# First stage of a three-layer attention kernel: turning normalised tokens on TensorE, loading tokens ahead of scalars, and putting value groups among key groups

## The reference, cut to what matters

```python
x = x + attn_a(layernorm(x))      # 8 heads, two 64-wide halves each
x = x + ffn(layernorm(x))         # int4-quantised kernel plus low-rank part
x = x + attn_b(layernorm(x))      # 16 heads, causal, rotary
x = x + ffn(layernorm(x))

# start of attn_a
q = xn @ Wq.T;  k = xn @ Wk.T;  v = xn @ Wv.T
q1, q2 = l2norm(q halves);  k1, k2 = l2norm(k halves)
# scalars: exp(sum(lq1*lk1)) - exp(sum(lq2*lk2)) + 0.5, 15*sigmoid(raw)*(1 + 0.5*tanh(delta))
# ffn: scale = max|kernel| / 7;  w = clip(round(kernel / scale), -8, 7)
```

## Time and profile before

| | |
|---|---|
| median of 3 runs | 1904.44 us (1903.51 to 1906.38) |
| profiled execution, time | 1904.92 us |
| its span on the slowest core (core 3) | 1903.4 us |
| spans of the 8 cores | 1889.3 to 1903.4 us |
| PE busy over the span | 1492.5 us (78%) |
| ACT busy | 1273.5 us (67%) |
| DVE busy | 1169.7 us (61%) |
| POOL busy | 511.6 us (27%) |

### The profile page before, as it was taken

One profiled execution on the slowest core, in us unless ns is written; L12 is line 12 of the kernel. 1 busy time (PEld: TensorE's weight loads), 2 busy tenths in 40 slices (PEclk: granted clock), 3 DMA queues, 4 the chain that ended last, 5 costly groups with the idle time before them and its releaser, 6 DMA issues.

```text
span 1903.4 us, 39272 instructions; the slowest of 8 cores (1889.3 to 1903.4 us)
## 1 busy us (share of the span) xinstructions
PE 1492.5 (78%) x13024; PEld 754.7 (40%) x13024; DVE 1169.7 (61%) x2158; ACT 1273.5 (67%) x1699; POOL 511.6 (27%) x1054
## 2 busy tenths in 40 slices
PE   0467997678888888888888885459788589888987
PEld 0123443444444444444444443124233234343443
DVE  2235467989989998999998996322433343423214
ACT  1254656888989989898988996013222568787990
POOL 1000002444444444444444444222433100000000
PEclk9989998989999999999999998789999589999988
DMA  9721502111011011101111010860200513131302
GB/s 188 95 51 34 125 4 85 55 52 28 29 34 45 29 44 35 30 27 39 41 35 44 29 34 23 147 118 1 45 1 0 106 32 106 36 101 24 95 18 70
DMA packets 137528, 101.52 MB, mean 53 GB/s; under 512 B 107747, under 2 KB 122211, under 8 KB 137078
## 3 DMA queue, kind: packets, MB, share of 16 engines
q1 hardware_dynamic: 121302, 84.20, 17.0%
q0 software_dynamic: 16032, 14.81, 5.4%
HBM read 67.65 MB, written 20.97 MB: 47 GB/s over the span
## 4 chain that ended last, share of the span: by engine, by line
PE 26%; ACT 17%; DVE 16%; issue 14%; POOL 7%; DMA 3%; SPq 1%; DVEq 0%; POOLq 0%; ACTq 0%
ACT E L175 9%; DVE Sx L184 8%; PE pBb L164 6%; PE pS L166 4%; PE pYb L171 4%; ACT EB L175 3%; ACT Gt L175 3%; PE pqb L164 3%; PE pY L171 3%; PE pB L164 3%; DVE ro L184 2%; POOL Q L184 2%; PE pL L166 2%; POOL K L184 2%; PE pD L164 1%
## 5 line engine op out<-in xcount | busy, mean ns | idle before, releaser
L184 DVE TENSOR_TENSOR Sx<-pL,Gt 128x512 f32<-128x512 f32 x1024 | 649.2, 682 | 75.0 <-PE pL L166 41.8
L175 ACT ACTIVATE E<-Sx 128x1024 bf16<-128x1024 f32 x512 | 541.7, 1058 | 51.0 <-DVE Sx L184 48.6
L171 PE MATMUL pY<-V,E 128*128 128x129 bf16 x4096 | 310.9, 222 | 88.9 <-ACT E L175 77.4
L175 ACT ACTIVATE EB<-pS,cst 128x1024 bf16<-128x1024 f32 (+1 forms) x320 | 296.6, 988 | 82.7 <-PE pS L166 80.2
L175 ACT ACTIVATE Gt<-pD 128x512 bf16<-128x512 f32 x512 | 304.4, 594 | 39.1 <-PE pD L164 37.3
L171 PEld LDWEIGHTS pY<-V,E 128*128 128x128 bf16 x4096 | 240.4, 98 | 197.5 <-issue 197.5
L164 PE MATMUL pD<-Qn,K 128*128 128x256 bf16 x1024 | 197.4, 274 | 45.1 <-ACT Gt L175 39.4
L166 PE MATMUL pL<-Q,K 64*128 64x256 bf16 x2048 | 203.2, 277 | 10.0 <-DVE Sx L184 9.9
L175 ACT ACTIVATE qb<-pqb 128x512 bf16<-128x512 f32 x64 | 38.2, 598 | 202.0 <-PE pqb L164 202.0
L184 DVE TENSOR_TENSOR ro<-pqb,x 128x512 f32<-128x512 f32 x64 | 44.2, 692 | 171.1 <-ACT qb L175 53.3
L171 PE MATMUL pYb<-V,EB 128*128 128x65 bf16 x2176 | 134.7, 202 | 10.0 <-DVE EB L184 4.8
(11 more groups left out here) (149 smaller groups left out, 1953.4 us busy)
## 6 DMA issues: line engine op xcount, KB each, us to landing
x<-xN SPq DMA_DIRECT2D x32, 512.0 KB, 4.5
x<-x SPq DMA_DIRECT2D x32, 512.0 KB, 3.2
out<-x SPq DMA_DIRECT2D x16, 512.0 KB, 2.6
x<-fker SPq DMA_DIRECT2D x3, 2048.0 KB
x<-WoT SPq DMA_DIRECT2D x2, 2048.0 KB
xn<-xn SPq DMA_DIRECT2D x16, 256.0 KB, 2.1
w_q<-WqT POOLq DMA_DIRECT2D x2, 1024.0 KB, 21.6
w_k<-WkT POOLq DMA_DIRECT2D x2, 1024.0 KB, 44.4
```

Source lines behind the costliest of these rows:

```text
L171: q.add(lambda e: e.matmul(out, lhsT, rhs, start=first, stop=last, skip_group_check=True))
L175: q.add(lambda e: e.activation(out, in_, func, **kw))
L184: q.add(lambda e: e.tensor_tensor(out, a, b, op))
```

## The change

1. Tiles 0 and 1 (blocks 0 to 7) are turned on TensorE by the new `turn_pe`: 8 matmuls of a 128x128 piece of `wq` with an identity matrix `ident`, four into each of two new PSUM banks `pT`, and a copy out of each, the first by ACT and the second by DVE. Tiles 2 and 3 are still turned by DMA.
2. The two banks come from `pqk`, which has 4 instead of 6 in this stage (`QK_BANKS`); the later projections keep 6 (`QB_BANKS`).
3. SP loads blocks 0 and 1, then the scalars, then blocks 2 and 3.
4. The scalars are computed behind `ln1(0..3)` and `turn_pe(4)` instead of ahead of them.
5. POOL issues `blk` and `ident` ahead of the weights.
6. In the first pair one V group follows each K group of tile 1 (8 among them, 8 behind); in the second pair one follows every second K group of tiles 2 and 3 (8 among them, 8 behind).

The core of the diff:

```diff
-QK_BANKS = 6
+QK_BANKS = 4
+QB_BANKS = 6
...
+    sl_c[0].start(po, blk[:, :], di["blk"])
+    c_tok = sl_c[0].start(po, ident[:, :], di["ident"])
...
+    load_x1(0)
+    load_x1(1)
     for i, n in enumerate(("lamq1", "lamk1", "lamq2", "lamk2")):
         bcast(sc[:, 64 * i:64 * (i + 1)], n, 64)
...
+    load_x1(2)
+    load_x1(3)
...
+    def turn_pe(n):
+
+        for _ in range(n):
+            b, a_tok = late_turn.popleft()
+            t, tb = b // 4, b % 4
+            toks = []
+            pe.wait(a_tok)
+            for k, q in enumerate((ac, ve)):
+                pe.wait(pT_free[k])
+                for c in range(4):
+                    col = 128 * (4 * k + c)
+                    mm(pe, pT[k][:, 128 * c:128 * (c + 1)], wq[:, b % 8, col:col + 128],
+                       ident[:, :], True, True)
+                q.wait(pe.done())
+                out = xn[t % 2][:, 4 * k:4 * k + 4, 128 * tb:128 * (tb + 1)]
+                if q is ac:
+                    act(ac, out, blocks_of(pT[k][:, :], 4), AF.Copy)
+                else:
+                    copy(ve, out, blocks_of(pT[k][:, :], 4))
+                pT_free[k] = q.done()
+            xt[b] = (pT_free[0], pT_free[1])
...
     ln1(range(0, 4))
-    turn_ln1(4)
+    turn_pe(4)
+
+    ac.add(lambda e: e.preload_act_table_set("exp_and_others"))
...
+        for t in (t0, t1):
+            for h in range(HA):
+                group_qk(Q, W3[0], w_tok[0:2], t, True, h)
+                if pair == 0 and t == t0 and h % 2 == 1:
+                    ln1([4 + h // 2])
+                    turn_pe(1)
+                if pair == 1:
+                    next(quant, None)
+        for t in (t0, t1):
+            for h in range(HA):
+                group_qk(K, W3[1], w_tok[2:4], t, False, h)
+                if pair == 0 and h % 2 == 1:
+                    ln1([8 + 4 * (t - t0) + h // 2])
+                if pair == 1:
+                    next(quant, None)
+                if (pair == 0 and t == t1) or (pair == 1 and h % 2 == 1):
+                    next_v()
+        while todo_v:
+            next_v()
```

More of the change, by code:

```diff
@@ L281, in build_program @@
     dram_in("sinbs", (128, T))
-    for w in ("tri", "perm", "blk"):
+    for w in ("tri", "perm", "blk", "ident"):
         dram_in(w, (128, 128))
@@ L437, in build_program @@
     pss = [ps(f"pss{i}", p1) for i in range(2)]
+    pT = [ps(f"pT{i}", p1) for i in range(2)]
     sqb = [sb(f"sqb{i}", (128, QT), BF16, s1) for i in range(2)]
@@ L469, in ln1_apply @@
         xm = wq[:, b % 8, :]
-        ve.wait(r_tok, xt.get(b - 8))
+        ve.wait(r_tok, *xt.get(b - 8, ()))
         ts(ve, xm, x[:, b % 4, :], st[:, b, 12:13], OP.subtract, st[:, b, 14:15], OP.mult)
@@ L474, in ln1_apply @@
             sy.wait(a_tok)
-            x_tok[b + 4] = sl_x[b % 4].start(sy, x[:, b % 4, :], rows_of(di["xN"], b + 4))
+            load_x1(b + 4)
         late_turn.append((b, a_tok))
@@ L535, in group_qk @@
         bank = pqk[bi]
-        pe.wait(pqk_free[bi], wt[h // 4], *[xt[4 * t + tb] for tb in range(4)])
+        pe.wait(pqk_free[bi], wt[h // 4], *[k for i in range(4) for k in xt[4 * t + i]])
         for c in range(NCH):
@@ L549, in group_v @@
         bank = pqk[bi]
-        pe.wait(pqk_free[bi], wt[hf], *[xt[4 * t + tb] for tb in range(4)])
+        pe.wait(pqk_free[bi], wt[hf], *[k for i in range(4) for k in xt[4 * t + i]])
         for c in range(NCH):
@@ L610, in quantize @@
                 yield 0
-                ve.wait(ve.done(), xt[8 + 4 * hf + i])
+                ve.wait(ve.done(), *xt[8 + 4 * hf + i])
                 ts(ve, wq[:, 4 * hf + i, :], x[:, i, :], -8.0, OP.max)
@@ L623, in build_program, with next_v @@
         t0, t1 = 2 * pair, 2 * pair + 1
[L624 to L634, removed]
-        todo_v = deque((t, hf, tb) for t in (t0, t1) for hf in range(2) for tb in range(4))
[L636 to L648, removed]
+        todo_v = deque((t, hf, tb) for t in (t0, t1) for hf in range(2) for tb in range(4))
+        def next_v():
             t, hf, tb = todo_v.popleft()
             group_v(W3[2], w_tok[4:6], t, hf, tb)
-            if pair == 1:
-                next(quant, None)
             if hf == 1 and tb == 3:
@@ L1075, in build_program @@
     p3 = contextlib.ExitStack()
-    pqk = [ps(f"pqb{i}", p3) for i in range(QK_BANKS)]
+    pqk = [ps(f"pqb{i}", p3) for i in range(QB_BANKS)]
     pss = [ps(f"psw{i}", p3) for i in range(2)]
```

93 lines of the change are left out of this document (46 added, 47 removed).

## The result

The changed kernel took 1892.01 and 1893.40 us against 1905.16 us for the kernel before on the same chip (median of four, 1903.51 to 1906.38): a ratio of 0.9935, 95% interval 0.9911 to 0.9959, or 12.4 us less. The forecast was 21.6 us less, and a time of 1883. The profiled execution took 1892.01 us with a span of 1890.5.

A forecast was written before the change was run, and what follows sets the result against it. Stage 1 counts: PE waits for turning DMAs and, among keys, for ACT behind DVE's statistics. -33.8 + 13.7 - 9 + 7.5 = -21.6 us against 1904.9 gives 1883.3, forecast 1883 us, range 1869 to 1894.

The forecast's parts named there:

- the highest pair: Two rivals combined, PE slow longer in tile 0 (1888) and late blocks (+3.8 us); pairs were said to reach 1893.
- front, first Q group: Start of stage 1: first Q group at 33.6 us instead of 67.4, -33.8 us.
- Q of tile 0, tile 1 less first group: Tile 0's queries: norm, turn and groups form a closed chain of 12.9 us a period, +13.7 us (+6.8 to +18.8).
- keys and values of the first pair: First pair: V groups among tile 1's keys fill PE's waits for norms; 18 us of stalls fall to 9, -9 us.
- banks and second pair: Second pair: with four banks DVE's wait for the ffn maximum reaches PE, +7.5 us (0 to 9).
- behind the stage: Everything after stage 1 stays word for word and only moves with the stage's end: 0 us.
- blocks 2 and 3 land no earlier: Rival at the front: these loads gain nothing over before, +3.8 us, 1887 us; chance 0.10.
- The copies out of `pT`: Front, behind the four norms: each round of copy, four matmuls and hand-over takes 1.4 us, 5.0 us in all.
- PE stays fast: Rival in tile 0: the clock stays up, period 10.6 us, 1876 us; chance 0.13.
- PE stays slow through h3: Rival in tile 0: the second group behind each turn is slow too, period 14.6 us, 1888 us; chance 0.17.
- three of them and the start of the fourth stay: Tile 0's keys, first pair: of the stalls at norms, some 2.5 us each, 8 us remain.
- anything behind stage 1 changes its length: Sign of being wrong: a changed length of any part after stage 1, which was taken as fixed.

The follow-up runs named there:

- old_load: The changed kernel, but SP issues the scalar transfers ahead of all four token blocks, as before the change; 1890.7 us (one run).
- old_front: The changed kernel, but scalars are loaded ahead of the blocks and computed ahead of the norms, as before the change; 1889.9 us (one run).
- w_late: The kernel before, but POOL issues the w_k and w_v loads only once tile 0's four DMA turns have landed; 1885.7 us, ratio 0.9894.
- banks6: The changed kernel, but from tile 1 on the two `pT` banks join the four `pqk`, so six rotate; 1886.1 us, ratio 0.9893.
- late_turn: The changed kernel, but in tile 0 the turns of blocks 4, 5 and 6 stand one Q group later; 1882.7 us, ratio 0.9878.
- best2: The changed kernel with turns two groups later, six banks, tile 0's keys ahead of tile 1's queries, a V behind every first-pair K group; 1857.3 us, ratio 0.9731.
- dma_turn1: The changed kernel, but blocks 4 to 7 are turned by DMA again, blocks 0 to 3 still on TensorE; 1880.4 us, ratio 0.9832.

## Why the prediction was right, and where it was not

Direction and range held, and the mechanism but for one step among the keys and a cause in the front; the time came out 9 to 10 us above the forecast. That it is inside the range is in part luck: 1892.7 lies 1.3 us below the upper end of 1894, and that end was set for pairs of rivals that did not come true (the highest pair, 1888 and 3.8 us more, gives 1892, not the 1893 that I wrote). Term by term on core 3, as start less start in the traces before and after:

| term | predicted | measured |
|---|---|---|
| front, first Q group | -33.8 | -33.1 |
| Q of tile 0, tile 1 less first group | +13.7 | +14.3 (52.90 less 38.63) |
| keys and values of the first pair | -9 | -6.1 (70.59 less 76.69) |
| banks and second pair | +7.5 | +7.9 (99.1 less 91.2) |
| stage end | -21.6 | -17.3 |
| behind the stage | 0 | +4.4 on the slowest core |

The four measured terms sum to -17.0 and not to -17.3, since tile 1's Q groups (17.57 against 17.78 us) are in none of them and the rest is rounding.

- **Front: the size was right and a cause was wrong.** I had blocks 2 and 3 take the place of blocks 0 and 1 behind the scalars. `old_load` and `old_front` show that neither the loads' order nor the scalars' place matters: the rival "blocks 2 and 3 land no earlier" describes what the order does. That block 3 was normed 3.5 us sooner on core 3 (25.72 against 29.22) is in part scatter among cores; the medians differ by 2.1 us, and with both edits undone by 1.5. My 25.4 us for these statistics was right by luck. The turn on TensorE carries the term, because it does not stand behind the weights' transfers (`w_late`).
- **The copies out of `pT`.** I took 1.4 us for a round; the rows give 1.53 (starts 29.67 and 31.20 on core 3). Right.
- **Q of tile 0: right, for the reason given.** Periods of 12.1, 12.9 and 13.2 us against 12.9. The rival "PE stays fast" fell: each period has 6 us of idle PE and a group of 3.17 to 3.62 us behind. "PE stays slow through h3" came in part: 1.89, 2.04 and 2.42 us for that group. A missed term is 0.94 us ahead of tile 1: a Q group needs block 7's copies out of `pT`, not only its turn.
- **Keys and values: the step that failed is "three of them and the start of the fourth stay".** The three cost 7.5 us as forecast (104.73 to 127.79 is 23.06 us, eight groups of 1.94 are 15.5). The fourth stayed whole, although a V group does stand ahead of the `pss` that waits for it:

```profile
127.57 0.38 PE L165 MATMUL pss<-sqb,c_blk 128*128 128x512 bf16 x1 [0.82 <-ACT sqb L176]
127.79 1.89 PE L165 MATMUL pqk<-xn,w_k 128*128 128x512 bf16 x8
...
129.77 1.89 PE L165 MATMUL pqk<-w_v,xn 128*128 128x512 bf16 x8
134.12 0.38 PE L165 MATMUL pss<-sqb,c_blk 128*128 128x512 bf16 x1 [2.47 <-ACT sqb L176]
```

`group_v` writes all pending rests right behind its own matmuls. So that `pss` now comes ahead of the second key group of tile 1, where it had stood behind it: between two waits PE has a key and a V group instead of two key groups, and nothing more to do than before. From the next norm on there are two key and two V groups between waits, and only 0.68 us is left (at 142.45). The forecast had 0.5 us for the fourth; it took 2.47. That is 2.0 of the missing 2.9 us, and the rest are pieces of under 0.7 us each behind it.
- **Banks: right, size too.** 5.85 us idle against 5.2, and a slow group of 3.57. That six banks hid the trip wholly was so on core 3 and three others; on the other four cores of the kernel before PE stood 0.2 to 1.5 us.
- **Behind the stage.** The prediction set the change against the profiled execution's slowest core and took the rest as fixed. The rest lies up to 11 and 13 us apart among the cores, and here 4.4 us of it went against the change; the medians of the rest are 1.2 us apart, so my sign of being wrong, "anything behind stage 1 changes its length", is not shown to have come true. By stage ends and ratios of the other kernels with several runs (`banks6` -21.4 and -20.4; `w_late` -20.4 and -20.2; `late_turn` -24.3 and -23.2; `best2` -51.4 and -51.2) the stage's gain passes through to the time; `dma_turn1` (-27.1 and -32.0, interval 18.9 to 45.0) is too wide to tell. That the changed kernel kept only 12.4 of 16.2 us is within the interval of its ratio (7.8 to 17.0 us).
- **The Trainium skill's figure for a turn.** The Trainium skill ("VectorE: DVE Perf Modes", section on the three transpose paths) gives 390 ns for one 128x128 piece. The trace does not bear it out for eight in a row: they took 1.01 us at 1.2 GHz and 0.61 at 2.4 GHz, as the rows of 129 columns had said, and not the 3.1 us of the estimate.

Left open: what held back SP's issues and the turns themselves while the weights were in flight. `w_late` shows that it was these loads, not by which path. A kernel that has `best2` and also the weights late was not tried.

## What to carry to other kernels

A long wait for a transfer at the start may be a matter of what is queued ahead of it: move the bulk loads first (here one wait on POOL, 20 us), then the work to another engine. When work moves into the list of an engine that had been free while waiting, ask which closed chain it joins: with the turns right behind the norms, tile 0 took 14.3 us longer than before; two groups later it took 36.7 us, as long as in the kernel before (36.8, both on core 1). And taking buffers away cost nothing where outputs came at an even pace, and much at the one long wait: the price is that wait less the cover that the buffers left.

## What the runs showed of the hardware

- Four turning DMAs of 256 KB with four weight loads in flight landed 35.0 us after the last norm (67.40 less 32.4, core 3), of which SP's issues alone took 26.13; without these loads, 10.6 us after it (43.76 less 31.45 + 1.69, core 7), with 8.19 of issues.
- Eight 128x128 turning matmuls take 1.01 us at 1.2 GHz and 0.61 at 2.4 GHz, with 1.53 us for a round of eight with the copy of 0.69 us.
- One load order gave block 3 at times 4.7 us apart on the eight cores (23.3 to 28.0 us), more than the order itself moved.
- With 24 matmuls in each of four waits of 6 us TensorE stayed at 2.4 GHz; four times 5.34 us of useless work took 9.2 us off the stage.
